# Who issues the loads of the next layer's weight chunks: GpSimd behind its splits, or SyncE in its order

## The reference

```python
for i in range(DEPTH):                 # DEPTH = 6, 16 heads of 64, window 32
    x = attn_layer(shift_tokens(x), Wqkv[i], q_scale[i], k_scale[i], Wo[i]) + x
    x = ffn_layer(shift_tokens(x), ln_g[i], ln_b[i], W1[i], b1[i], W2[i], b2[i]) + x

def attn_layer(x, Wqkv, qs, ksc, Wo):
    q, k, v = split(x @ Wqkv)          # to heads
    q, k = l2norm(q) * qs, l2norm(k) * ksc
    q = q * cos * scale + rotate_half(q) * sin * scale
    k = k * cos / scale + rotate_half(k) * sin / scale
    return merge(local_attention(q, k, v)) @ Wo
```

## Time and profile before

| | us |
|---|---|
| median of 3 runs | 1957.35 |
| lowest and highest of the runs | 1952.11, 1962.66 |
| the profiled execution | 1964.37 |
| its span, first to last instruction | 1963.1 |
| TensorE busy | 1860.7 |
| ScalarE busy | 1595.7 |
| VectorE busy | 1577.5 |
| GpSimd busy | 1071.2 |

### The profile page before, as it was taken

One profiled execution on the slowest core, in us unless ns is written; L12 is line 12 of the kernel. 1 busy time (PEld: TensorE's weight loads), 2 busy tenths in 40 slices (PEclk: granted clock), 3 DMA queues, 4 the chain that ended last, 5 costly groups with the idle time before them and its releaser, 6 DMA issues.

```text
span 1963.1 us, 77055 instructions
## 1 busy us (share of the span) xinstructions
PE 1860.7 (95%) x34029; PEld 1563.9 (80%) x34029; DVE 1577.5 (80%) x2234; ACT 1595.7 (81%) x2751; POOL 1071.2 (55%) x523
## 2 busy tenths in 40 slices
PE   6999999868999999999999999999999999999987
PEld 4889889757888888888888788887888887887866
DVE  3556665488888898989889798988888888988873
ACT  2678887667888988888888789888888989888864
POOL 4100000266667675777666775757766677766530
PEclk9999999989999999999999999999999999999998
DMA  6000000023434334343443433443434334333431
GB/s 176 12 7 5 5 7 7 2 83 95 115 102 115 100 103 112 99 128 98 120 116 83 128 103 107 108 115 104 127 106 109 96 105 114 104 107 87 113 85 36
DMA packets 120102, 173.89 MB, mean 89 GB/s; under 512 B 25591, under 2 KB 44634, under 8 KB 119770
## 3 DMA queue, kind: packets, MB, share of 16 engines
q1 hardware_dynamic: 119596, 168.92, 31.3%
q10 hardware_dynamic: 174, 0.05, 0.0%
HBM read 117.54 MB, written 51.38 MB: 86 GB/s over the span
## 4 chain that ended last, share of the span: by engine, by line
PE 65%; POOL 11%; DVE 10%; ACT 8%; issue 6%; DMA 0%; ACTq 0%; POOLq 0%; SPq 0%; DVEq 0%
PE o_pair L765 7%; PE bank L713 6%; POOL rt L1704 6%; PE bank L845 6%; PE s_pair L735 5%; PE bank L690 5%; PE bank L692 4%; PE bank L691 4%; PE bank L617 4%; POOL rt L1695 3%; PE bank L747 3%; DVE bank L1491 3%; PE bank L867 2%; DVE t L1504 2%; PE bank L779 2%
## 5 line engine op out<-in xcount | busy, mean ns | idle before, releaser
L1704 POOL TENSOR_TENSOR rt<-rt,t 128x2048 f32<-128x2048 f32 x96 | 440.1, 4584 | 154.3 <-DVE t L1504 149.9
L1695 POOL TENSOR_TENSOR rt<-raw,rot 128x1024 f32<-128x1024 f32 x192 | 456.3, 2377 | 34.7 <-ACT raw L1026 12.9
L690 PE MATMUL bank<-wqkv_hi,xs 128*128 128x512 f32 x576 | 256.3, 445 | 14.2 <-ACT vn L1043 8.7
L1026 ACT ACTIVATE raw<-bank 128x512 f32<-128x512 f32 x384 | 223.5, 594 | 31.1 <-PE bank L692 18.4
L1512 DVE TENSOR_TENSOR rt<-rt,bank 128x2048 f32<-128x2048 f32 x96 | 219.7, 2288 | 29.9 <-POOL rt L1704 27.7
L765 PEld LDWEIGHTS o_pair<-pT,v 64*64 64x64 f32 x12288 | 195.3, 135 | 45.5 <-issue 20.3
L692 PE MATMUL bank<-wqkv_hi,xs 128*128 128x512 f32 x576 | 230.0, 399 | 0.0
L691 PE MATMUL bank<-wqkv_lo,xs 128*128 128x512 f32 x576 | 229.1, 398 | 0.0
L1504 DVE TENSOR_TENSOR t<-raw,bank 128x1024 f32<-128x1024 f32 x192 | 225.1, 1214 | 0.6
L1491 DVE TENSOR_REDUCE bank<-t 128x32 f32<-128x2048 f32 x96 | 219.5, 2287 | 7.5 <-ACT t L1034 4.6
L713 PE MATMUL bank<-const,rt 128*128 128x128 f32 x1536 | 217.1, 279 | 7.2 <-DVE rt L1512 5.7
(11 more groups left out here) (403 smaller groups left out, 4319.1 us busy)
## 6 DMA issues: line engine op xcount, KB each, us to landing
v<-v_rows SPq DMA_DIRECT2D x288, 256.0 KB, 4.5
v_rows<-vn SPq DMA_DIRECT2D x192, 256.0 KB, 2.6
v<-v_rows SPq DMA_DIRECT2D x96, 192.0 KB, 3.2
wraw<-in_L_ffn_Wqkv_dram SPq DMA_DIRECT2D x36, 256.0 KB, 2.9
wo<-in_L_ffn_Wo_dram SPq DMA_DIRECT2D x24, 128.0 KB, 2.8
wraw<-in_L_ffn_W_in_dram SPq DMA_DIRECT2D x8, 256.0 KB, 2.7
w_out<-in_L_ffn_W_out_dram SPq DMA_DIRECT2D x8, 256.0 KB, 3.0
wraw<-in_L_ffn_W_dram SPq DMA_DIRECT2D x12, 170.5 KB, 2.3
```

Of the source, the lines that this page charges most:

```text
L690: pe.matmul(bank[:, :], hi, w[0][:, :], start=True, stop=False)
L1026: act.activation(k.raw_r[c][:, n * 512:(n + 1) * 512], k.one.at["qk", j][:, :], ACT.Copy)\
L1695: e = pool.tensor_tensor(heads(k.rt_r[c][:, part]), heads(k.raw_r[c][:, part]), cosv, ALU.mult)
L1704: pool.tensor_tensor(k.rt_r[c][:, :], k.rt_r[c][:, :], k.t2[:, :], ALU.add).then_inc(s["rot_add"], 1)
```

## The change

Only who issues the loads of later chunks changes, and at which place of which stream. Chunks up to `BY_SP` (the experts' eight, all of layer 0 and the first two of layer 1) are loaded by SyncE as before, with the semaphores `ld_chunk0` and `ld_chunk1`. All later ones, 38 loads, are issued by GpSimd in `split(n)`, right behind the split of chunk i-2, on two semaphores of their own, `ld_next0` and `ld_next1`, and `split_chunk` waits on these. `next_chunk` and its slots w0 to w7 go from SyncE's stream.

```diff
-SP_AT = dict(gain=5, w0=33, w1=74, w2=79, w3=79, st00=79, st01=81, st10=88, st11=88, w4=88, pair00=90, pair01=107,
-             w5=107, pair10=119, pair11=128, wo=166, w6=201, w7=201, w2d=222)
+SP_AT = dict(gain=5, st00=79, st01=81, st10=88, st11=88, pair00=90, pair01=107, pair10=119, pair11=128, wo=166, w2d=222)
...
+BY_SP = NE + NCHUNK_LATE + 2
...
     def split_chunk(i, hi, lo):
         src = k.wraw[i % 2][:, 0:k.chunk_width(i)]
-        pool.wait_ge(s[f"ld_chunk{i % 2}"], 16 * (i // 2 + 1))
+        if i < BY_SP:
+            pool.wait_ge(s[f"ld_chunk{i % 2}"], 16 * (i // 2 + 1))
+        else:
+            pool.wait_ge(s[f"ld_next{i % 2}"], 16 * ((i - BY_SP) // 2 + 1))
...
         def split(n):
+
             if next_layer:
                 split_weights(l + 1, n)
+                i = NE + NCHUNK_LATE * (l + 1) + n + 2
+                if i < k.n_chunks:
+                    pool.dma_start(*k.chunk_load(i)).then_inc(s[f"ld_next{i % 2}"], 16)
...
-    for i in range(NE, NE + 2 + NCHUNK_LATE):
+    for i in range(NE, BY_SP):
         load_chunk(i)
...
-        def next_chunk(n):
-            if next_layer:
-                load_chunk(NE + NCHUNK_LATE * (l + 1) + n + 2)
...
-        for n in range(4):
-            yield from t.to(f"w{n}")
-            next_chunk(n)
...
-        yield from t.to("w4")
-        next_chunk(4)
...
-        yield from t.to("w5")
-        next_chunk(5)
...
-        yield from t.to("w6")
-        next_chunk(6)
-        yield from t.to("w7")
-        next_chunk(7)
```

More of the change, by code:

```diff
@@ L212 @@
     "ld_ident ld_x0 ld_x1 ld_x2 ld_x3 ld_first ld_rows ld_wmod0 ld_wmod1 ld_w0 ld_const ld_chunk0 ld_chunk1 ld_moe ld_out0 ld_out1 "
-    "ld_gain0 ld_gain1 ld_wo ld_w2 v2_0 v2_1 st_v0 st_v1 st_out").split()
+    "ld_gain0 ld_gain1 ld_wo ld_w2 v2_0 v2_1 st_v0 st_v1 ld_next0 ld_next1 st_out").split()
 NU = DEPTH * B
```

## The result

The changed kernel takes 1975.69 us (median of 4 runs, 1972.03 to 1976.66) where the kernel before took 1956.28 beside it (1952.11 to 1962.66). The ratio is 1.0076, with a 95% interval of 1.0055 to 1.0097: 14.9 us more (10.8 to 19.0). The two medians lie farther apart, 19.4 us (a ratio of 1.0099, just beyond that interval); the text goes by the ratio of 1.0076, and so 14.9 is known to a few microseconds only. The profiled executions show less than that, spans of 1970.7 against 1963.1 us, because the one of after was the fastest of its runs and the one of before slower than any of its others. So the two traces are compared here by units, not by their ends.

What follows compares the result with a forecast made beforehand. Steady units were taken as TensorE's, weight-split units as held by GpSimd's work ahead of the adds. Terms 5.0 (w1) + 10.0 (w2, w3) + 2.0 (w6) = 17.0 us took the median from 1957.35 to 1974.4 us; range 1960 to 2004.

Steps and rivals of the forecast that it cites:

- Where it is paid: Issues behind w0, w4, w5, w7 covered by GpSimd's idle time; those behind w1, w2, w3, w6 paid.
- The price T: GpSimd's time per load issue, estimated at 1.0 us for a plain chunk and 1.2 for a v chunk.
- The terms: Costs by place of issue: w1 5.0 us, w2 and w3 10.0, w6 2.0.
- the slack of 0.42: Behind w2 and w3: 0.14 us before the second add plus 0.28 behind it, subtracted from two v-chunk issues per turn.
- the step that could fail: Forecast wrong if ScalarE and VectorE absorb the second add's delay before it reaches TensorE.
- The clock: Rival: longer TensorE waits behind w1 and w3 lower its clock, ten times 1.4 us, 14 us more: 1988.4 us; chance 0.12.
- the plain sum: Exposed issues behind w1, w2/w3 and w6 add to 17.0 us, without clock falls; chance of this forecast 0.55.
- SyncE's freedom: Gain from freeing SyncE taken as 0; rival: pauses inside o_pair products vanish, -6.8 us, 1950.6 us; chance 0.05.
- The dear v chunk: Rival: GpSimd's cost grows with row pieces, 4.2 us per v chunk; 46.9 us more, 2004.3 us; chance 0.08.
- the cheap issue: Rival: GpSimd hands each transfer on in 0.35 us as SyncE does; 3.2 us more, 1960.5 us; chance 0.17.
- the lock: Rival: GpSimd's issue waits for the VectorE instruction in flight at 19 exposed issues; 22 us more, 1996 us; chance 0.03.
- What would show it: Signs in the changed trace: later first add, longer ScalarE and TensorE waits, w1's unit 36.0 us, 1.2 us idle behind w5.

Runs made afterwards that it cites:

- the early split: Against the kernel before, all loads on SyncE: an eighth pair of split-weight buffers lets w1's split move ahead of xs; ratio 0.9973, 5.3 us faster.

## Why the prediction was right, point by point

The forecast was 1974.4 us and slower; it came to 1975.69, a ratio of 1.0087 expected by the medians and 1.0076 measured. The 17.0 us of the sum lie between the 14.9 of the measured ratio and the 19.4 of the medians. By its steps:

**Where it is paid: right.** Covered places cost nothing (1.0003), exposed ones the whole (1.0085), and memsets of about the same length lose as much (1.0093). The list of covered places, read from the idle time behind each split, held for all four.

**The price T: right by luck of the mean.** The geometric mean between 0.35 us and the landing gave 1.0 and 1.2. Measured in the order: 0.83 (0.60 to issue it, 0.30 to wait for the split, less 0.07) and 1.15. The pieces of a v chunk cost 0.33 us more, not 3. The 0.30 us was in no row of before. The Trainium skill's figure of about 1 us to the first byte ("DMA: Bandwidth & Descriptors", Specifications) had given 14.9 us by that estimate, and 14.9 is what the measured ratio gives. No row here shows a first byte, though, and what the order pays is another quantity (0.58 us held and 0.30 waited), so the agreement is no proof of the page.

**The terms.** w1: 5.0 forecast, 5 x 0.83 = 4.1 at full clock. w2 and w3: 10.0 forecast, 5 x 2.0 = 10.0; the slack of 0.42 in it is 2.30 - 2.0 = 0.3. w6: 2.0 forecast, 0.66 in the one turn where it can be read, so at most 4 x 0.66 = 2.6 if the others are alike; the time cannot tell it from 0. That the delay of the second add would reach TensorE was named as the step that could fail, and it held: 1.78 us of wait where there was none.

**The clock: the step that was wrong.** I gave it as a rival, as if either it or the plain sum would come. Both came. All five turn units of after had a fall, and in the kernel with w1's load alone the falls make more than half of what its turn units cost (9.4 against 4.1). The rival's own sum was wrong too. It added 1.4 us to each of ten waits; a turn had one fall at most, worth 1.1 us (34.85 against 33.77) to 2.7 us (36.48 against 33.77) where w1 alone is late, and only 0.1 to 0.9 us in the four turns of after where it stood behind the first add and the second add was late as well (36.40 against 35.79 in the second), since TensorE then works slowly through a wait that it would have had. Only where the fall came behind the second add did it cost about the rival's 1.4 us (36.42 against 34.95). So the 16.4 us of the turn units are 14.2 at full clock and only 2.2 more: the fall and the second add's delay cover each other, and that the plain sum held in spite of five falls is this cover, which the prediction did not have. That units of after also won something back outside the turns (13.2 us more over the 45 units from the first one on, 8.5 with the 46th, against 16.4 in the turn units) is luck on top. A fall met the kernel before three times there (twice in its second profile), after once; with falls as chancy as above that is no effect of the change that could be claimed.

**SyncE's freedom: 0, as taken.** The pauses of the o_pair products did shrink, from 10.0 (8.9 in the second profile of before) to 5.9 us, and the longest from 2.7 to 1.1; also where GpSimd has only the covered loads (7.9). But those of the other rows grew: all pauses with no releaser but "issue" on TensorE from 560 us on make 13.2 us in before (11.8 in its second profile) and 12.5 in after. Whether the move gives a microsecond or two is below what the intervals can tell.

**The dear v chunk, the cheap issue, the lock.** 0.91 us against the 4.2 or 0.35 of the first two. The third: the issues average 0.706 and 0.599 us over 38 of them, beside a VectorE that is busy for 80% of the span, with instructions of up to 2.29 us. One by one, the plain ones take 0.58 to 0.60 us (one 0.70) and those of v chunks 0.91 or 0.92 at all five turns, where a wait for whatever is left of a VectorE instruction would be expected to vary. So the trap of which the Trainium skill warns ("SBUF — State Buffer", the box on the DVE-blocks-DMA trap) did not show, with the mix of VectorE instructions that runs here.

**What would show it.** Forecast and found: gap ahead of the first add 1.1 us, 0.91; ScalarE's wait 3.0, 2.85; TensorE's 2.8, 2.57; the unit 36.0, found 35.78 at full clock and 36.40 with a fall; idle time behind w5 1.2, 1.33. In the first turn the two waits behind w1 were absent, because a pause of 1.9 us that ended at 601.58 had held TensorE and ScalarE up before; the second add's delay alone came through (1.20 us).

**What stays open.** The kernel with w2's and w3's loads alone costs 17.6 us and all eight cost 14.9, w1 alone 10.0: they don't add up as times, while the full-clock units do (0.83 + 2.0 = 2.84). By the medians it is 15.2, 19.4 and 7.2 us, so that two loads cost more than all eight is not shown either. The two intervals overlap (13.1 to 21.9 and 10.8 to 19.0). What decides whether a wait of 1.75 us brings a fall, never in 15 units of two kernels and in 9 of the 18 others, isn't settled. Nor is what brings the pauses without a releaser, two of which stood right ahead of a fall in a turn unit (1.90 us in after, 2.66 us with the early split).

## What to carry to other kernels

Before work is put on an in-order engine, ask at each of its places how long the engine idles behind it: here 19 of 38 loads were free, the four behind w6 cost 0.66 us or so each at most, and 15 paid their price. Price a delay on a path to TensorE as the wait plus a possible clock fall, and don't add both for every wait: a later delay in the same unit can be paid out of the slow stretch. And a place where added work costs in full is one where work taken away gains: moving w1's split out of it made the kernel 5.3 us faster (2.0 to 8.4).

## What the runs showed of the chip that I had not expected

- A load issued by GpSimd holds it for 0.58 to 0.60 us for a plain chunk (128 rows in one piece each) and 0.91 us for a v chunk (1024 pieces), and its issue begins 0.30 us after the end of the split ahead of it (0.07 us for a computing instruction). The chunks also land later. The first row is of the page of after; the second is SyncE's, of the page of before, whose 36 loads are the same 28 and eight that stand before 300 us in both kernels (KB, median us to landing; the 28 alone have 2.9 too):

```profile
wraw<-in_L_ffn_Wqkv_dram POOLq DMA_DIRECT2D x28, 256.0 KB, 3.5
...
wraw<-in_L_ffn_Wqkv_dram SPq DMA_DIRECT2D x36, 256.0 KB, 2.9
```

- With 0.8 us more of one wait of TensorE, its clock falls far more often behind it: 17 of 20 waits of 2.2 to 2.6 us, 9 of 33 of 1.4 to 1.8 us. A fall lasts 3 to 10 us at 1.2 GHz and makes TensorE's busy time in the unit 1.2 to 4.2 us longer (4.2 for the falls of 10 us in the kernel with memsets).
